# Four spectral layers on one core: the last inverse transform on eight 32x64 tiles in bursts of 32 rows

## The reference

```python
def full_layer(x, w1, b1, w2, b2):        # layers 0, 2 and 3 (scale factors left out)
    xs = rfft2(x, axes=(1, 2))            # (2, 64, 33, 384), complex
    xs = xs.reshape(2, 64, 33, 8, 48)     # 8 blocks of 48 channels
    o1 = relu(xs @ w1 + b1)               # complex product, relu on both parts
    o2 = softshrink(o1 @ w2 + b2, 0.01)
    return irfft2(o2) + x

def layer_1(x):
    h = x + afno(layernorm(x)) + layernorm(x)   # 32 x 32 of the modes are kept, gelu, no shrink
    m = layernorm(h)
    return gelu(m @ mlp_w1 + mlp_b1) @ mlp_w2 + mlp_b2 + h
```

## Time and profile before

| | |
|---|---|
| median of 3 executions | 2065.68 us (2064.65 to 2067.0) |
| span of the profiled execution | 2057.0 us |
| TensorE busy | 1919.2 us, 93% |
| VectorE (DVE) busy | 1173.7 us, 57% |
| ScalarE (ACT) busy | 1008.7 us, 49% |
| GpSimd (POOL) busy | 435.4 us, 21% |

### The profile page before, as it was taken

How to read it: one execution, slowest core, us unless ns; L and a number is a source line. 1 busy time by engine, 2 the same in 40 slices (tenths; PEclk the granted TensorE clock), 3 DMA queues, 4 the chain that set the end, 5 groups by cost and what they waited for, 6 DMA issues and landing times.

```text
span 2057.0 us, 68971 instructions
## 1 busy us (share of the span) xinstructions
PE 1919.2 (93%) x31104; PEld 1570.9 (76%) x31104; DVE 1173.7 (57%) x2480; ACT 1008.7 (49%) x1644; POOL 435.4 (21%) x425
## 2 busy tenths in 40 slices
PE   4999995698998999999999999999899999999996
PEld 3777772576776999999999999999777777777774
DVE  3687887977855433333333333332377767677675
ACT  3766545576753333333333333333466666665652
POOL 3212104965631000000000000000221211221200
PEclk9999997799999999999999999999999999999998
DMA  9425738307434111111111111114532573557314
GB/s 164 100 49 85 129 62 142 55 4 129 114 86 122 32 31 31 31 31 31 31 31 31 31 31 31 31 31 73 94 53 49 87 127 80 84 99 126 60 40 96
DMA packets 299701, 141.05 MB, mean 69 GB/s; under 512 B 275760, under 2 KB 298032, under 8 KB 299440
## 3 DMA queue, kind: packets, MB, share of 16 engines
q1 hardware_dynamic: 299440, 137.08, 36.2%
HBM read 74.14 MB, written 62.91 MB: 67 GB/s over the span
## 4 chain that ended last, share of the span: by engine, by line
PE 80%; DVE 9%; SPq 3%; ACT 2%; issue 2%; POOL 2%; DMA 1%; DVEq 0%; POOLq 0%; ACTq 0%
PE ps L693 20%; PE ps L678 19%; PE ps L586 8%; PE ps L523 8%; PE ps L537 7%; PE ps L602 6%; PE ps L555 5%; PE ps L504 4%; DVE u L937 3%; DVE st L974 2%; SPq L357 1%; DVE xs L962 1%; PE ps L565 1%; DMA wraw<-in_w 1%; PE ps L663 1%
## 5 line engine op out<-in xcount | busy, mean ns | idle before, releaser
L1086 DVE TENSOR_TENSOR gl<-g,gh 128x512 fp32r<-128x512 f32 x192 | 156.8, 816 | 476.3 <-ACT gh L872 476.3
L937 DVE TENSOR_TENSOR u<-ps,clamp 64x192 f32<-64x192 f32 (+1 forms) x864 | 378.1, 438 | 27.7
L869 ACT ACTIVATE g<-ps,colp 128x512 f32<-128x512 f32 x192 | 132.3, 689 | 529.1 <-PE ps L678 529.1
L523 PEld LDWEIGHTS ps<-const,z 128*48 128x48 f32 x8384 | 266.0, 124 | 134.9 <-issue 128.6
L732 ACT ACTIVATE z<-ps 64x512 f32<-64x512 f32 x366 | 234.9, 642 | 155.1 <-PE ps L504 148.2
L523 PE MATMUL ps<-const,z 128*48 128x64 f32 (+1 forms) x8384 | 270.3, 217 | 10.2 <-issue 5.3
L1173 POOL COPY xn<-xs 128x512 f32<-128x512 f32 x144 | 152.0, 1096 | 535.8 <-PE ps L504 343.9
L693 PE MATMUL ps<-w2h,gh 128*128 128x384 f32 x768 | 261.9, 341 | 0.0
L693 PE MATMUL ps<-w2h,gl 128*128 128x384 f32 x768 | 258.6, 337 | 0.0
L693 PE MATMUL ps<-w2l,gh 128*128 128x384 f32 x768 | 257.5, 335 | 0.0
L586 PEld LDWEIGHTS ps<-const,u 128*64 128x64 f32 x6144 | 206.7, 139 | 52.2 <-issue 25.7
(11 more groups left out here) (70 smaller groups left out, 2463.4 us busy)
## 6 DMA issues: line engine op xcount, KB each, us to landing
after<-xs SPq DMA_DIRECT2D x96, 384.0 KB, 5.4
xs<-after SPq DMA_DIRECT2D x94, 384.0 KB, 8.8
after<-om SPq DMA_DIRECT2D x32, 384.0 KB, 4.3
out<-xs SPq DMA_DIRECT2D x32, 384.0 KB, 5.5
xm<-after SPq DMA_DIRECT2D x30, 384.0 KB, 6.3
xs<-in_x SPq DMA_DIRECT2D x24, 384.0 KB, 8.4
wstage<-in_spectral SPq DMA_DIRECT2D x16, 210.0 KB, 5.8
xs<-in_x SPq DMA_DIRECT2D x4, 768.0 KB, 11.9
```

What stands on the lines that cost most here:

```text
L523: mm = pe.matmul(ps[a * SIDE:a * SIDE + BLOCK, F2_BANK, n * L.kh:(n + 1) * L.kh], z[:, g % 2, slot, :], basis(col + a * SIDE, L.kh), start ...
L937: dve.tensor_tensor(u[to, g % 2, :, start + b:start + size:BATCH], whole, limited, ALU.subtract).then_inc(u_ready, 1)
L1086: dve.tensor_tensor(gl[:, n % 4, :], g[:, n % 2, :], gh[:, n % 4, :], ALU.subtract).then_inc(g_low, 1)
```

## The change

`f6` is rebuilt. Its contraction of 128 partitions is split into quarters of 32, and `v` is laid out by image, `v[P, 2, BATCH, SIDE, TWO]`, with the two halves of 24 channels on different partitions. A burst is 32 rows; a block has two. Each burst is two steps of eight matmuls (four row groups of 32 partitions, each with two column halves); each step writes four banks, and step 1, after a wait for step 0 (`f6_half`), adds to them. So a block has 32 matmuls of 384 columns instead of 16. A burst takes the banks of `f1` and `f5`, `BURST_BANKS`, `f5` gets two banks, and the sum on DVE takes two banks in one instruction, four instructions a block instead of eight.

`u` is laid out by image too, without the two extra slots. The 33rd mode gets a path of its own: DVE writes it to `last` (four small instructions), `f5_last` on TensorE transforms it (two matmuls), DVE copies the result to `turned_last`, and four DMAs issued by ACT (`place_last`) move it across partitions into one row of `v` for each image and half. The first burst of the block waits for them (`v_whole`).

The places move: in full layers bursts stand in slots 8 (first, block g-1) and 1 (second, block g-2), `f1` in 2, 4, 6 and `f5` in 2, 3, 4, 5, 6, 6. In layer 1 both bursts stand in slot 0, and `f1` goes ahead of `f2`, one slot later. The row statistics are taken out of the sum's function and have a table of slots.

```diff
-AHEAD = 3
+AHEAD = 2
-        self.f1_at = [0, 3, 6] if self.full else [0, 1, 2]
-        self.centre_at = [0, 0, 1, 2, 2, 3]
-        self.f5_at = [2, 3, 4, 5, 6, 7] if self.full else [1, 1, 2, 2, 3, 3]
+        self.f1_at = [2, 4, 6] if self.full else [1, 2, 3]
+        self.centre_at = [0, 1, 1, 2, 3, 3]
+        self.f5_at = [2, 3, 4, 5, 6, 6] if self.full else [1, 1, 2, 2, 3, 3]
...
-def rows_at(g, t):
+def bursts_at(g, t):
 
     if not layer_of(g).full:
-        return [(g - 2, 2 * t), (g - 2, 2 * t + 1)]
-    if t == layer_of(g).n - 1:
-        return [(g - 1, 0)]
-    return [(g - 2, t + 1)] if t < ROWCHUNKS - 1 else []
+        return [(g - 2, r) for r in range(BURSTS)] if t == 0 else []
+    return {1: [(g - 2, 1)], layer_of(g).n - 1: [(g - 1, 0)]}.get(t, [])
+
+
+STATS_AT = {0: (0, 1), 2: (2,), 3: (3,), 4: (4,), 5: (5,), 6: (6,), 7: (7,)}
...
-            v = sb("v", [P, 2, SIDE, BLOCK])
+            v = sb("v", [P, 2, BATCH, SIDE, TWO])
...
+            def f5_last(g):
+
+                pe.wait_ge(last_ready, 2 * BATCH * full_before(g + 1))
...
+                for b in range(BATCH):
+                    mm = pe.matmul(ps[b * SIDE:(b + 1) * SIDE, bank, LAST_AT:LAST_AT + BLOCK],
+                                   basis(C_D5 + SIDE, SIDE), last[:, g % 2, b, :], start=True, stop=True)
+                mm.then_inc(last_done, 1)
...
+                for step in range(2):
+                    if step:
+                        pe.wait_ge(f6_half, BURSTS * g + r + 1)
+                    for n, bank in enumerate(burst_banks(g, r)):
+                        part, half = n // 2, n % 2
+                        a = part ^ step
+                        quadrant = slice((2 * a + half) * HALF, (2 * a + half + 1) * HALF)
+                        rows = slice(r * BURST_ROWS + part * BURST_PART, r * BURST_ROWS + (part + 1) * BURST_PART)
+                        for b in range(BATCH):
+                            mm = pe.matmul(ps[b * SIDE:(b + 1) * SIDE, bank, 0:BURST_PART * TWO],
+                                           const[quadrant, column:column + SIDE],
+                                           v[quadrant, g % 2, b, rows, :].rearrange("p h c -> p (h c)"),
+                                           start=step == 0, stop=step == 1)
+                    mm.then_inc(f6_done if step else f6_half, 1)
...
+            def place_last(g):
+
+                act.wait_ge(v_ready, CHUNKS * (g + 1))
+                act.wait_ge(last_kept, full_before(g + 1))
+                for b in range(BATCH):
+                    for j in range(2):
+                        row = SIDE + j * HALF
+                        act.dma_start(v[row:row + 1, g % 2, b], turned_last[b * SIDE:(b + 1) * SIDE, g % 2, j * TWO:(j + 1) * TWO]
+                                      ).then_inc(v_whole, 16)
...
                         if L.full:
+                            if t == L.f5_at[-1] + 1 and g > first:
+                                place_last(g - 1)
                             for k in late:
                                 f1(g + 1, k, PIECES[2:3])
                         if t:
                             m1(g - 1, layer_of(g - 1).n - 1)
...
+                for part, bank in enumerate(burst_banks(g, r)[::2]):
+                    to = residual(g, r * BURST_ROWS + part * BURST_PART)
+                    dve.tensor_tensor(to, ps[:, bank:bank + 2, 0:BURST_PART * TWO].rearrange("p j (h c) -> p j h c", c=TWO),
+                                      to, ALU.add).then_inc(res_ready, 1)
```

More of the change, by code:

```diff
@@ L46 @@
 C_D2, C_D2A, C_D2B, C_SIGN = [SPAN + P * n for n in range(4)]
[L47 removed]
+C_ID, C_D5, C_D5H, C_D6 = [C_SIGN + SIGNS + P * n for n in range(4)]
+C_COLS = C_D6 + 2 * SIDE
+TWO = BLOCK // 2
 ROWS = ONE_ROW + 1
@@ L111, in imag_of, with segment_of, full_before @@
     return sum(BATCH for g, _ in GROUPS[:count] if layer_of(g).norm)
[L114 to L131, removed]
+def segment_of(g):
+    return [segment for segment in SEGMENTS if segment[0] <= g][-1]
+def full_before(g):
+    return sum(layer_of(n).full for n in range(g))
 def shrunk_before(g):
@@ L551, in m2 @@
                 if L.full:
+                    if t == LAST_SLOT and g > segment_of(g)[0]:
+                        f5_last(g - 1)
                     for c in range(size):
@@ L617, in spectral @@
                             m1(g - 1, layer_of(g - 1).n - 1)
-                        rows = [r for r in rows_at(g, t) if r[0] >= first]
+                        bursts = [r for r in bursts_at(g, t) if r[0] >= first]
                         ahead = at_slot(L.f1_at, t) if g + 1 < last else []
@@ L823, in spectral @@
                         if not L.full:
-                            for k in late:
-                                f1(g + 1, k, PIECES[2:4])
+                            for k in ahead:
+                                f1(g + 1, k, PIECES[0:2])
                         f2(g, t)
@@ L831, in spectral @@
                                 f1(g + 1, k, PIECES[0:2])
[L832 removed]
+                        else:
+                            for k in ahead:
+                                f1(g + 1, k, PIECES[2:4])
+                        for k in behind:
                             f5(g - 1, k)
[L834 to L841 removed]
                         if L.norm and t:
@@ L852, in spectral @@
                 for k in range(CHUNKS):
-                    f5(g, k, LAST_BANKS[k % 2])
+                    f5(g, k)
+                if layer_of(g).full:
+                    place_last(g)
             def turn(r, i, k):
@@ new lines, in m2, with f5_last @@
+                    offset = lnrow[0:1, 1, block * BLOCK:(block + 1) * BLOCK].rearrange("p (j t) -> p j t", j=2)
+                    for b in range(BATCH):
+                        mean = u[0:1, g % 2, b, :, :, 0].rearrange("p t j -> p j t")
+                        dve.scalar_tensor_tensor(mean, offset, float(SIDE), mean, ALU.mult, ALU.add).then_inc(u_ready, 1)
+            def f5_last(g):
+                dve.wait_ge(last_done, full_before(g + 1))
+                if full_before(g) >= 2:
+                    dve.wait_ge(v_whole, LAST_MOVES * (full_before(g) - 1))
+                dve.tensor_scalar(turned_last[:, g % 2, :], ps[:, last_bank(g), LAST_AT:LAST_AT + BLOCK], layer_of(g).inverse, None,
+                                  ALU.mult).then_inc(last_kept, 1)
@@ new lines, in row_statistics @@
+            def row_statistics(g, k):
+                last = g >= BLOCKS - 2
+                if g % 2 == 0 and not last:
+                    return
+                dve.wait_ge(res_ready, PARTS * g + k // 2 + 1)
+                if g == 1 and k == 0:
+                    dve.wait_ge(wpart_high, WPARTS)
+                for r in range(k * ROWCHUNK, (k + 1) * ROWCHUNK):
+                    data = xs[buffer_of(g // 2)][:, r, :]
+                    if last:
+                        data = data[:, g % 2 * BLOCK:(g % 2 + 1) * BLOCK]
+                    dve.bn_stats(st[:, r, g - PAIRS + 1 if last else g // 2, :], data).then_inc(st_done, 1)
+                if g == BLOCKS - 1:
+                    dve.wait_ge(st_done, (STATS - 1) * SIDE + (k + 1) * ROWCHUNK)
+                    for r in range(k * ROWCHUNK, (k + 1) * ROWCHUNK):
+                        dve.bn_aggr(mv[:, r, :], st[:, r].rearrange("p a b -> p (a b)")).then_inc(mv_ready, 1)
@@ L1032, in spectral @@
                             m2(g - 1, layer_of(g - 1).n - 1)
+                        for r in bursts[1:]:
+                            f6(*r)
                         if norm:
```

230 lines of the change are left out of this document (116 added, 114 removed).

## The result

The changed kernel takes 2151.49 us (median of 4, 2149.92 to 2155.16), the kernel before in the same comparison 2065.16 (2061.49 to 2067.0). The ratio is 1.0416, with an interval of 1.0394 to 1.0437. It is 86 us slower; 2083 was forecast, and 2110 was the upper end of the range. The profiled spans differ by 92.6 us, 2149.6 against 2057.0.

A forecast was written before the change was run, and what follows sets the result against it. TensorE, busy for 93% of the span, was taken as the bound. Terms -19 + 3 + 37 + 4 - 6 + 1.5 - 2 = +18.5 us on the 2057.0 span, plus 8.7 carried over, gave 2084, stated as 2083; range 2040 to 2110.

The forecast's parts named there:

- its term for the stall: Slot 7: TensorE's m2 waits 1.75 us for h behind four ACT DMA issues, in 21 blocks, +37 us.
- All of d is lost: Slot 7: the length d of each ACT DMA issue stalls TensorE uncovered, S = 0.1 + 4d.
- I take the shortest: ACT's DMA issue in slot 7 priced by SP's shortest kind, 0.37 us plus a gap, d = 0.41 us.
- Late landing: Rival: ACT's DMAs land after 4.8 us behind SP's loads, burst waits 1.3 us more in 21 blocks, +27, 2110; chance 0.09.
- The burst: New f6 on TensorE: two steps of eight matmuls on eight tiles, 1.95 us each, bounds 1.45 and 3.2.
- The gain per block: Full block on TensorE: 5.2 - 3.9 - 0.12 - 0.15 = 1.0 us won, the 0.15 for less cover in slot 0.
- The 0.09 us: Tile shape change in front of f1: f6 takes 0.74 us there against 0.65.
- the term -19: Full blocks 18 to 31 and 2 to 6, 19 blocks with both bursts and TensorE as the bound: -19 us.
- Layer 1: Bursts gain nothing net; fewer centring calls ahead of the first f5, partly offset by other waits: -6 us.
- The odd blocks of layer 0: Blocks 3 and 5: row statistics on DVE in slot 0 delay the burst's sums and f1, +4 us.
- Blocks 1 and 17: These blocks get a burst in place of one call, +1.4 us each, +3 in all.
- The end: End of layer 3: burst waits 3.4 us for v, issues and landing, and first stores go out later, +1.5 us.

The follow-up runs named there:

- no_moves: The changed kernel without the four DMAs of place_last and the waits for them (33rd mode's row left out): 2075.26 us, 1.0045 of before.
- after_paced: The changed kernel, complete, with SP's stores and loads of units 8 to 12 spread over slots: 2142.1 us, 1.0381 of before.
- before_four_dmas: The kernel before with four more DMAs on ACT, read by nobody, at the head of slot 7 in 15 blocks of layers 2 and 3: 2108.17 us, 1.0199.
- two_moves: The changed kernel with two of the four DMAs, image 1's two rows left out: 2107.17 us, 1.0219 of before.
- issues_only: no_moves with four DMAs on ACT into a dead tile at place_last's place in blocks 17 to 31: 2109.78 us, 1.0214 of before.

## Why the prediction was wrong, point by point

**Two parts of the miss.** no_moves splits it. Without its term for the stall the forecast gives 2046 us; no_moves takes 2075, 29 more. For the four DMAs the forecast gives 37 us; they cost 76, 39 more. The 2083 would also have been 2084 by its own sum.

**The mechanism of the stall was right, and its term was too small.** "All of d is lost" holds. With d = 0.41 the stall was to be 1.75 us; an issue took 0.47 the first time and 0.62 after it, 2.42 for four, and the stall measured 2.34, inside the bounds of 0.1 and 2.6. That is the step "I take the shortest": the second kind of the earlier trace rows, 0.59, was the right neighbour. 0.6 us more in 21 blocks are +12 us. The Trainium skill's 50 ns for the sequencer's dispatch (DMA: Bandwidth & Descriptors, Anatomy of one DMA), given there for GpSimd's path, doesn't price a DMA issue on ACT: the trace has 470 to 620 ns of held queue. Its section Issuing engines are not separate DMA queues says that the time to initiate a DMA is usually small relative to the DMA itself. Here one issue takes 0.47 to 0.62 us of the 1.8 to 1.9 from issue to landing, about a third, and the four issues one behind the other, 2.42 us, are all of the cost in a quiet block.

**What follows the stall was missing altogether.** First, the clock: the mean granted clock is 0.956 in the changed kernel and 0.968 in no_moves. In blocks 1 to 6 and 17 to 30 it falls to 0.50 fifteen times in the changed kernel and five times in no_moves, ten falls more. At 1.6 us each they cost about 16 us. The rest of the difference lies in the drains, where TensorE is partly idle anyway. The waits for `h` differ by 45.5 us between the two (49.5 and 4.0), and the burst's waits with no releaser by 15.4 (16.7 and 1.3). The three together are 77 us, an estimate, against 76 between the medians and 72 between the profiled spans. The sum counted what a stall takes, and not what the stretch behind it takes. The page TensorE: Matmul & The Clock Gate (Part 1: The HAM clock gate) of the Trainium skill says that an idle TensorE is put back to 1.2 GHz. The rows at 2072 agree, and the stalls of the same length without a fall show that the stall alone doesn't decide it.

Second, some issues take longer than 0.62 us, up to 1.58 in the changed kernel. The expectation of after_paced puts this down to SP issuing at the same time. The traces don't bear that out: of eight such issues in layers 2 and 3 four have an issue of SP beside them, and four stand in blocks in which SP issues nothing for over 8 us around, as here; ten others with an issue of SP beside them took 0.47 to 0.62. The cause stays open.

```profile
1596.48 3.38 ACTq L855 DMA_DIRECT2D v<-turned_last  x4
...
1601.31 1.36 PE L579 MATMUL ps<-w,h 113*64 113x96 f32 x16 [3.29 <-ACT h L823]
```

**Late landing** was a rival with 0.09 and a price of 27 us. It came true in part, on top of the forecast: in four loading blocks the last row took 6.3 to 6.9 us to land, and the burst waited 6.6 us in all.

**The burst** was to cost 1.95 us and costs 1.86 to 1.87, plus 0.11 that the `f2` in front of it takes longer. This term was right, and eight tiles do work together. The gain per block, 1.0 us, was not: a quiet block of no_moves takes 34.1 us against 34.6. The 0.09 us that `f6` took longer in front of `f1` didn't go with `f6`. It sits in front of `f1` whatever stands there: in no_moves `f2` costs 0.99 instead of 0.89 us at that place, three times a block. And `m2`, `m1` and `f2` in slots 0, 7 and 8 take 0.6 us longer without cover, where 0.15 was allowed. By the quiet blocks the term -19 should have been about -10.

**A sign was wrong in the loading blocks.** The -19 was given to all 19 blocks, and in those with SP's transfers nothing is won: 39.1 us against the 36.2 of the kernel before. SP's stores came in four pairs before, 6 to 10 us apart, because `f6` finished its rows bit by bit; a burst frees two parts at once, so stores, weights and loads follow each other nearly without a gap for 30 us, and TensorE's instructions come beside them on the same 16 DMA engines. Such waits for "issue" were there in the kernel before too (7.8 us in layer 1, below), and the prediction didn't ask what they were.

**Layer 1** was to give -6 and costs +10 in blocks 8 to 14, also in no_moves (+11). The 7.65 us in front of the first `f5` are gone, as said. In their place stand a wait of an early `f1` for the centring on DVE, which the prediction had only as "other waits come forward", the waits of bursts for DVE, and more stops with no releaser:

```profile
412.43 1.99 PE L526 MATMUL ps<-const,xn 64*64 64x64 f32 x64 [4.33 <-DVE xn L1070]
```

TensorE's waits in the stretch behind it, after (425 to 620 us) and in the kernel before (410 to 596 us):

```profile
PE ps L654 <- DVE xs L1033: 8.9, 6, 2.4
PE ps L623 <- issue: 7.0, 4, 3.0
PE ps L545 <- issue: 3.7, 3, 2.0
```

```profile
PE ps L504 <- issue: 7.8, 4, 2.6
PE ps L586 <- ACT v L795: 2.9, 5, 1.6
```

**Smaller terms.** The odd blocks of layer 0 were to lose 4 us to row statistics; in no_moves blocks 3 and 5 win 1.3 and 0.5 us. Blocks 1 and 17 lose 4.8 and 1.3 in no_moves, +3 was said. The start of the kernel wins 4.9 to 6.2 us up to block 0's first `h`, since `f1` of block 1 comes two slots later; I hadn't looked there. But by the end of block 1 nothing is left of it (+0.1), so the wait seems only to have moved there. The end was to cost +1.5 and costs 6.6 with block 31: the landing as computed, the issues 2.41 us instead of 1.64, and then both bursts at clock 0.50, 3.3 us each instead of 1.93:

```profile
2124.98 2.41 ACTq L855 DMA_DIRECT2D v<-turned_last  x4
2128.76 3.29 PE L654 MATMUL ps<-v,const 32*64 32x384 f32 x32 [4.46 <-issue]
```

The range was too narrow at its upper end. A stall of 2.6 us in 21 blocks alone gave 2102, and late landing on top of it 2129. The two don't exclude each other and should have been added; even so, the clock and the loading blocks were missing.

## What to carry to other kernels

A DMA issued by ACT cost it 0.47 to 0.62 us here, in the middle of its work, and at times up to 2.2: give each its own gap, or put it on a queue that nobody waits for. That alone isn't enough: both took the stall away here, and these kernels still took 43 to 46 us more than the one before, for the rows then landed late beside SP's loads. Where TensorE is the bound and is unrolled, its instructions compete with the data, as these traces are read: spread large transfers over the block instead of queueing them. And price a stall of TensorE together with the stretch at half clock that can follow it: 2.3 us of stall cost up to 3.8 us of block here.

## What the hardware showed that I had not expected

- TensorE stops for up to 3.1 us in the middle of a group of matmuls, while SP's transfers keep the DMA share at 1.2 to 1.3; spacing the transfers removes most of it (39.1 to 35.6 us a block). That the missing thing is the instruction stream is read from the place of the stops and from the `q8` packets, 1.4 to 1.7 us behind whose end TensorE goes on. The profile doesn't say whose instructions `q8` carries, and no run moved that stream by itself.
- Of the changed kernel's 17 stalls of 2.3 us and more at this place, 11 were followed by a granted clock of 0.50, six weren't (2.34 us at 1919.8 for one). In before_four_dmas it was four of the eight of 2.6 to 3.4 us and none of the seven of about 1.7, in two_moves none of twelve of 1.04 to 1.1. In after_paced it was 14 of 19. Stalls of 1.9 us at this place had a fall behind them twice in issues_only and twice in after_paced. What tells a stall with a fall behind it from one of the same length without stays open.
- ACT's second DMA took 0.83 to 1.58 us instead of 0.62 in seven of the changed kernel's blocks, and its fourth 1.53 in another. SP was issuing beside it in four of the eight. In after_paced five issues took 0.85 to 1.35 us, and SP issued beside none of them. What holds the queue up isn't known.
